# A two-layer decoder on one core: the first loads of two of its attention stages asked for one stage ahead

## What is computed

```python
x = x + _L0_attn_ref(_layernorm(x, axis=-1), L0_attn_w_qkv, L0_attn_b_qkv, L0_attn_w_out, L0_attn_b_out)
x = x + _L0_xattn_ref(_layernorm(x, axis=-1), ctx_1024, ctx_1024, L0_xattn_W_out, L0_xattn_b_out)
x = x + _L0_ffn_ref(_layernorm(x, axis=-1), L0_ffn_Wg, L0_ffn_A, L0_ffn_B)
x = x + _L1_attn_ref(_layernorm(x, axis=-1), L1_attn_Wq, L1_attn_bq, L1_attn_Wk, L1_attn_bk, L1_attn_Wv, L1_attn_bv)
x = x + _L1_xattn_ref(_layernorm(x, axis=-1), ctx_1024, ctx_1024, L1_xattn_wq, L1_xattn_wk, L1_xattn_wv, L1_xattn_wo)
x = x + _L1_ffn_ref(_layernorm(x, axis=-1), L1_ffn_weight, L1_ffn_weight_scale, L1_ffn_bias)
```

## Time and profile before

| what | value |
|---|---|
| median of 3 executions | 3616.16 us |
| the three | 3609.43, 3616.16, 3617.14 us |
| the profiled execution's own time | 3610.95 us |
| its span, first to last instruction | 3609.2 us |
| PE busy, share of the span | 85% |
| DVE, ACT, POOL busy | 75%, 65%, 29% |
| DMA moved | 572.96 MB, mean 159 GB/s |
| expert stage, first DMA to first DMA of the next stage | 1279.53 to 1434.70 us |
| band stage, the same | 1434.70 to 1827.05 us |
| cross stage, the same | 1827.05 to 3427.93 us |

### The profile page before, as it was taken

The page is one execution under the profiler, slowest core; times in us unless marked ns, Lnnn a source line. Parts: engine busy times, 40 slices in busy tenths (PEclk is TensorE's granted clock), DMA queues, the critical chain, the costliest instruction groups (busy, mean ns, idle before and its releaser), DMA issues. The chain is left out here.

```text
span 3609.2 us, 78473 instructions
## 1 busy us (share of the span) xinstructions
PE 3069.9 (85%) x30984; PEld 1833.0 (51%) x31124; DVE 2697.0 (75%) x4017; ACT 2354.9 (65%) x4397; POOL 1062.7 (29%) x1854
## 2 busy tenths in 40 slices
PE   6999989968998944999958898998899989999824
PEld 3747474745665633444435554555555555555411
DVE  4848483767887855344459998889888989899688
ACT  3838383766876634333349988779877888788534
POOL 2232323056346334233322222222222222222122
PEclk9999999989998977999989999999999999999956
DMA  4050505074375175244489999999999999999843
GB/s 154 27 158 18 174 2 151 13 266 120 134 229 169 53 246 202 82 122 121 115 217 192 194 190 203 190 201 198 209 184 194 200 208 188 192 203 192 155 160 126
DMA packets 1308095, 572.96 MB, mean 159 GB/s; under 512 B 1144146, under 2 KB 1230802, under 8 KB 1305172
## 3 DMA queue, kind: packets, MB, share of 16 engines
q1 hardware_dynamic: 1303700, 551.16, 69.4%
q0 software_dynamic: 4032, 16.78, 1.2%
HBM read 174.19 MB, written 109.45 MB: 79 GB/s over the span
## 5 line engine op out<-in xcount | busy, mean ns | idle before, releaser
L2309 DVE TENSOR_REDUCE ca_neg_max<-banks 128x1 f32<-128x1024 f32 x512 | 624.1, 1219 | 82.6 <-PE banks L2087 81.0
L2317 DVE SCALAR_TENSOR_TENSOR ca_halves<-ca_probs,ca_inv,ca_halves 128x1024 f16<-128x1024 f32 x512 | 655.5, 1280 | 39.1 <-ACT ca_halves L2243 29.9
L2235 ACT ACTIVATE ca_probs<-banks,ca_neg_max 128x1024 f32<-128x1024 f32 x512 | 570.5, 1114 | 80.4 <-DVE ca_neg_max L2309 77.5
L2243 ACT ACTIVATE ca_halves<-ca_probs,ca_inv 128x1024 f16<-128x1024 f32 x512 | 587.1, 1147 | 15.8 <-DMA ca_pt<-ca_halves 14.9
L2053 POOL TENSOR_SCALAR ca_inv<-ca_total 128x1 f32<-128x1 f32 x512 | 98.4, 192 | 1153.2 <-ACT ca_probs L2235 1153.2
L2087 PE MATMUL banks<-ca_kt,ca_qt 64*128 64x512 f16 x3072 | 381.0, 381 | 34.3 <-ACT ca_probs L2235 32.8
L2109 PE MATMUL banks<-ca_pt,ca_v 128*64 128x256 f16 x6144 | 387.7, 276 | 16.4 <-DMA ca_pt<-ca_halves 16.2
L2109 PEld LDWEIGHTS banks<-ca_pt,ca_v 128*64 128x64 f16 x6144 | 319.0, 110 | 108.5 <-issue 88.9
L2056 POOL TENSOR_TENSOR ca_inv<-ca_inv,ca_minus_one 128x1 f32<-128x1 f32 x512 | 281.6, 550 | 42.6
L2087 PEld LDWEIGHTS banks<-ca_kt,ca_qt 64*128 64x128 f16 x3072 | 131.3, 95 | 224.6 <-issue 80.8
L2068 PE MATMUL banks<-ca_ct,ca_w 128*128 128x512 f16 x768 | 179.0, 383 | 38.2 <-DMA ca_ct<-ctx_part 23.6
(11 more groups left out here) (306 smaller groups left out, 5737.2 us busy)
## 6 DMA issues: line engine op xcount, KB each, us to landing
ca_w<-ca_w_parts SPq DMA_DIRECT2D x20, 768.0 KB, 5.3
wa_v<-v_rows SPq DMA_DIRECT2D x44, 264.0 KB, 4.6
v_rows<-wa_v_stage SPq DMA_DIRECT2D x32, 264.0 KB, 2.2
wa_x<-in_x SPq DMA_DIRECT2D x32, 256.0 KB, 4.8
wa_ring<-in_x SPq DMA_DIRECT2D x32, 256.0 KB, 3.6
x_after_window_attention<-wa_ring SPq DMA_DIRECT2D x32, 256.0 KB, 3.2
ba_tokens<-wa_tok_turned SPq DMA_DIRECT2D x32, 256.0 KB, 3.6
ba_xt<-ba_tokens SPq DMA_DIRECT2D x32, 256.0 KB, 7.6
```

The source lines that it names most:

```text
L2235: act.activation(probs[:, slot, :], scores(i), ACT.Exp, bias=neg_max[:, slot:slot + 1], accum_out=total[:, slot:slot + 1]).then_inc(exped, 1)
L2243: act.activation(halves[:, i % HALF_SLOTS, 0, :], probs[:, slot, :], ACT.Copy, scale=inv[:, slot:slot + 1]).then_inc(split_hi, 1)
L2309: dve.tensor_reduce(out=neg_max[:, slot:slot + 1], in_=scores(i), axis=X_AXIS, op=ALU.max, negate=True).then_inc(maxed, 1)
L2317: dve.scalar_tensor_tensor(out=halves[:, i % HALF_SLOTS, 1, :], in0=probs[:, slot, :], scalar=inv[:, slot:slot + 1], in1=halves[:, i % HAL ...
```

## The change

Two objects are allocated before the expert stage, in stacks of their own, so that they live across stages. `BandOpening` holds `wv`, its staging tile and the band stage's token tiles; `CrossOpening` holds the cross stage's token tiles, context tiles and weight slots. The expert stage's SP asks for `wv` behind its first residual rows (its batch 1 tokens now follow that), ACT and DVE split it in batch 0 of that stage, and SP asks for the band's first 8 token tiles ahead of the expert's last batch of stores. The band's SP asks for the cross stage's first loads ahead of its own last batch of stores. The two stacks are closed after the band and after the cross stage, each with a clear and a barrier. In the band stage `wq` and `wk` become weights 0 and 1, and the split of `wv` at the head of its ACT and DVE programs goes.

```diff
@@ expert_ffn, SP
                 for t in range(NT):
                     a.load(sp, 0, t)
                 for t in range(NT):
+                    load_residual(sp, n, x_in, 0, t)
+                consts.band.load(sp)
+                for t in range(NT):
                     a.load(sp, 1, t)
-                for t in range(NT):
-                    load_residual(sp, n, x_in, 0, t)
 
                 def before_stores(b, follows):
+                    if not follows:
+                        wait_first_batch_kept(sp, k)
+                        for t in range(NT):
+                            consts.band.a.load(sp, 0, t)
                     if b + 2 < B:
...
@@ expert_ffn, ACT
+                    if b == 0:
+                        consts.band.split_high(act)
@@ expert_ffn, DVE
+                    if b == 0:
+                        consts.band.split_low(dve)
                     out_projection_vector(dve, n, o, k, b)
...
+class BandOpening:
+    def __init__(self, sb, sem, dram):
+        self.source = dram["l1_wv"].rearrange("(k p) n -> p k n", p=P)
+        self.stage = sb("bd_wv_stage", [P, KC, D], F32)
+        self.wv = [sb(f"bd_wv{p}", [P, KC, D], F16) for p in range(2)]
+        self.a = Arrivals(sb, sem, "bd", dram["bd_tokens"])
+        self.loaded, self.high, self.low = sem("bd_wv_loaded"), sem("bd_wv_high"), sem("bd_wv_low")
+
+    def load(self, sp):
+        sp.dma_start(self.stage[:, :, :], self.source).then_inc(self.loaded, 16)
+
+    def split_high(self, act):
+        act.wait_ge(self.loaded, 16)
+        act.activation(self.wv[0][:, :, :], self.stage[:, :, :], ACT.Copy, scale=WS).then_inc(self.high, 1)
+
+    def split_low(self, dve):
+        dve.wait_ge(self.high, 1)
+        dve.scalar_tensor_tensor(out=self.wv[1][:, :, :], in0=self.stage[:, :, :], scalar=WS, in1=self.wv[0][:, :, :],
+                                 op0=ALU.mult, op1=ALU.subtract).then_inc(self.low, 1)
...
+def wait_first_batch_kept(sp, k):
+    for slot in range(k.slots):
+        sp.wait_ge(k.kept[slot], 16 * len(range(slot, NT, k.slots)))
...
@@ band_attention, SP
-                weights(0)
-                for t in range(NT):
-                    a.load(sp, 0, t)
...
-                for m in (1, 2):
+                for m in range(2):
                     weights(m)
...
+                def before_rows(b, follows):
+                    if not follows:
+                        wait_first_batch_kept(sp, k)
+                        consts.cross.open(sp)
...
@@ band_attention, PE
-                pe.wait_ge(w_lo, 1)
+                pe.wait_ge(consts.band.low, 1)
...
+class CrossOpening:
...
+    def open(self, sp):
+        self.load_weights(sp, 0)
+        for p in range(2):
+            self.load_context(sp, 0, p)
+        for t in range(NT):
+            self.a.load(sp, 0, t)
+        self.load_weights(sp, 1)
...
@@ program
+            if name == "expert_ffn":
+                cross_stack, cross_sb, cross_sem = scoped(nc)
+                consts.cross = CrossOpening(cross_sb, cross_sem, dram)
+                band_stack, band_sb, band_sem = scoped(nc)
+                consts.band = BandOpening(band_sb, band_sem, dram)
...
+            if name == "band_attention":
+                band_stack.close()
+            if name == "cross_attention":
+                cross_stack.close()
```

More of the change, by code:

```diff
@@ L77, in __init__ @@
         self.turn, self.x_turn = 0, 0
+        self.band, self.cross = None, None
 def constants(nc, sb, sem):
@@ L1586, in beside @@
                         a.load(sp, b + 1, t)
-                stream_rows(sp, n, x_in, x_out, k, beside=beside)
+                def before_rows(b, follows):
+                    if not follows:
+                        wait_first_batch_kept(sp, k)
+                        consts.cross.open(sp)
+                stream_rows(sp, n, x_in, x_out, k, before=before_rows, beside=beside)
             @block.gpsimd
@@ L1728, in sequence @@
                         if b == 0 and i == 2:
+                            weight_high(0)
+                        if b == 0 and i == 4:
                             weight_high(1)
-                        if b == 0 and i == 4:
-                            weight_high(2)
                         if b == 0 and i == VS:
@@ L1812, in sequence @@
                         if b == 0 and i == 2:
+                            weight_low(0)
+                        if b == 0 and i == 4:
                             weight_low(1)
-                        if b == 0 and i == 4:
-                            weight_low(2)
                         if b == 0 and i == VS:
@@ L1868, with __init__, load_context, pair_of @@
 EARLY_PAIRS = PAIRS - 2
+class CrossOpening:
+    def __init__(self, sb, sem, dram):
+        self.dram = dram
+        self.a = Arrivals(sb, sem, "ca", dram["ca_tokens"])
+        self.ct = [sb(f"ca_ct{p}", [P, KC, S], F16) for p in range(2)]
+        self.w = sb("ca_w", [P, W_SLOTS, 3, 2, KC, P], F16)
+        self.ct_loaded, self.w_loaded = sem("ca_ct_loaded"), [sem(f"ca_stream_loaded{i}") for i in range(W_SLOTS)]
+    def load_context(self, sp, b, p):
+        sp.dma_start(self.ct[p][:, :, :].rearrange("p k s -> p (k s)"),
+                     self.dram["ctx_parts"][p][b * P:(b + 1) * P, :]).then_inc(self.ct_loaded, 16)
+    def pair_of(self, turn):
+        b, at = divmod(turn, PAIRS)
+        return at if b % 2 == 0 else PAIRS - 1 - at
+    def w_place(self, turn):
+        return self.pair_of(turn) % W_SLOTS
+    def w_kept(self, turn):
+        return turn >= PAIRS and turn % PAIRS < W_SLOTS
+    def w_loads(self, turn):
+        return sum(1 for u in range(turn + 1) if self.w_place(u) == self.w_place(turn) and not self.w_kept(u))
+    def load_weights(self, sp, turn):
+        if self.w_kept(turn):
+            return
+        pair, place = self.pair_of(turn), self.w_place(turn)
+        sp.dma_start(self.w[:, place, :, :, :, :].rearrange("p m q k c -> p (m q k c)"),
+                     self.dram["ca_w"][pair * P:(pair + 1) * P, :]).then_inc(self.w_loaded[place], 16)
+    def open(self, sp):
[5 more added lines that the diff above has]
+        self.load_weights(sp, 1)
 def cross_attention(nc, consts, psum, x_in, x_out, dram):
@@ L1875, in cross_attention @@
         n = Residual(sb, sem, "ca", consts, psum)
[L1876 to L1878 removed]
         minus_one = sb("ca_minus_one", [P, 1], F32)
[L1880 to L1909 removed]
+        wo_loaded = sem("ca_wo_loaded")
+        early = consts.cross
+        a, ct, w, ct_loaded, w_loaded = early.a, early.ct, early.w, early.ct_loaded, early.w_loaded
+        pair_of, w_place, w_loads, load_weights, load_context = \
+            early.pair_of, early.w_place, early.w_loads, early.load_weights, early.load_context
         qt = [[sb(f"ca_qt{a}{p}", [P, S], F16) for p in range(2)] for a in range(2)]
@@ L1993, in _ @@
             def _(sp):
-                load_weights(sp, 0)
-                for p in range(2):
-                    load_context(sp, 0, p)
-                for t in range(NT):
-                    a.load(sp, 0, t)
-                load_weights(sp, 1)
                 for t in range(NT):
```

36 lines of the change are left out of this document (6 added, 30 removed).

## The result

| what | before | the change |
|---|---|---|
| executions timed first | 5 | 5 |
| their median | 3611.21 us | 3589.59 us |
| lowest to highest | 3605.95 to 3617.14 us | 3582.96 to 3597.13 us |
| the profiled execution's own time | 3610.95 us | 3588.61 us |
| all executions of this study | 82, mean 3613.3 us | 24, mean 3593.8 us |

The change is faster: 0.9934 of the time before, 95% interval 0.9919 to 0.9949, that is 18 to 29 us. Over all 24 executions of the change the mean is 3593.8 and the median 3595.1, both inside it. The gain in means is 3613.3 − 3593.8 = 19.5 us, with 2.4 us either way (single executions of either kernel scatter with a standard deviation of 5 us; twice √(5.3²/82 + 5.1²/24)). 16.9 were forecast.

A forecast was written before the change was run, and what follows sets the result against it. Most time lies inside stages, but PE's waits for opening loads at the band and cross edges count in full. 9.5 + 8.9 − 0.5 − 1.0 = 16.9 us off 3616.2 gives 3599 us, range 3590 to 3608.

The forecast's parts named there:

- Edge into the band: Band stage opening: with `wv` split and tokens on chip, PE waits only for the masks; gain 9.5 us.
- Edge into the cross stage: Cross stage opening: weights, context and tokens on chip, PE waits only for the barrier; gain 9.4 us before the extra close.
- The price of a start behind a barrier: Both stage openings: PE's delay with nothing else to wait for, between 0 and 0.7 us, taken as 0.1.
- Rival 2: Both stage openings: PE starts late behind the barrier, by 3.3 us; 11.4 us gained, 3605; chance 0.10.
- Extra closes: Ends of band and cross stages: each second stack's clear and barrier costs about 0.5 us.
- The split: Expert stage, batch 0: splitting `wv` on ACT and DVE delays residual adds; cost 1.0 us, between 0 and 1.92.
- Loads at no cost in the expert stage: Expert stage, SP and DMA: early `wv` and band token loads are covered; nothing, or a microsecond or two if cover fails.
- rival 1: Expert stage: 3.1 MB of moved loads lengthens the DMA-bound stage by 8.7 us, leaving 8.2 gained, 3608; chance 0.13.
- Twelve loads in the band's last batch at no cost: Band stage, SP: 5.8 MB of cross-stage loads fit into 39 us of slack before SP's next store; cost nothing.
- Rivals 3 and 4: Cross loop slowed by new tile addresses, 3625, chance 0.04; another wait replacing the loads at one opening, 3608, chance 0.03.
- The clock: Band and cross openings: PE's first products stay slow at granted clock 0.50 despite less idle time; counted as nothing.
- The range: Whole kernel: 3590 (18.9 gained off the lowest run, 3609.4) to 3608, which takes in three of the four rivals.

The follow-up runs named there:

- the third and fourth: The change itself, unedited, timed and profiled again beside the kernel before: medians 3595.70 us of 6 executions and 3598.84 us of 7.

## Why the prediction was right and where it was wrong

- **Edge into the band, −9.5.** Right: PE's first product moved from 10.68 us of the stage to 1.10, 9.6 us, held by the masks; forecast was 1.15. `wq` was not late. In the two profiles of the change whose clock falls as before, the third and fourth, the band stage is 9.8 us shorter (382.4 against 392.2), where 9.0 were forecast with the close.
- **Edge into the cross stage, −9.4.** Right: from 9.49 to 0.19, 9.3 us. The price of a start behind a barrier, bounded by 0 and 0.7 and taken as 0.1, measured 0.19. Rival 2 is out. No run here shows the fetch that the Trainium skill (Runtime: NRT & Kernel Launch, Instruction fetch mechanics) describes behind a taken branch: if there was one, it lies within these 0.19 us or ahead of the barrier, where PE waits anyhow. That such a fetch would now be exposed is not shown.
- **Extra closes, 0.5 each.** Nearly right. At the band's end the two semaphore clears start 0.7 us apart and the two barriers end 0.5 us apart. From PE's last product of the cross stage to the last stage's first instruction it takes 4.40 or 4.41 us in the seven profiles with a second close there and 4.02 or 4.03 in the four without, so that close costs 0.4 us:

```profile
L53 POOLq EVENT_SEMAPHORE_RANGE_CLEAR  x2: 91/221/351, 1814.7 to 1815.4; - x2
L54 SPq EVENT_SEMAPHORE  x2: 17/17/17, 1815.2 to 1815.7; - x2
```

- **The split, +1.0.** 0.6 by the means of five and eight profiles. Its working was right in kind: in the fourth profile the first add comes 1.6 us late (28.2 us), where 1.9 had been worked out, the second 0.5. At the last add of the stage 0.1 us is left there (142.05 against 141.91), 0.5 in the mean of all profiles.
- **Loads at no cost in the expert stage.** Right, and with it rival 1 is out. SP came to the last batch's stores at 131.2 us of the stage (1407.91), where 131.5 had been worked out, and the first keep slid by 1.4 us (by 2.0 to 3.9 in the other profiles with these loads), but the stage's end hardly did:

```profile
1403.98 3.88 SPq L163 DMA_DIRECT2D bd_xt<-bd_tokens  x6
1407.91 7.26 SPq L422 DMA_DIRECT2D x_after_expert_ffn<-ef_ring  x5
1415.47 0.56 SPq L303 DMA_DIRECT2D bd_tokens<-ef_tok_turned  x1
```

- **Twelve loads in the band's last batch at no cost.** Right: SP issued them from 1728.43 to 1739.53, its next store began at 1767.90.
- **Rivals 3 and 4** are out. From the first maximum to the last the cross loop takes 1541.3 us in the mean of seven profiles with the early opening and 1540.0 in the four with the old one, 0.005 us a step, where 0.066 would have eaten the gain. No other wait took over.
- **The clock: "I count nothing here".** Right on average (367.4 against 367.6 us from PE's first to its last product), but the forecast looked at the first products only, and these stay slow. That the falls of the clock later in the stage may come out otherwise in each execution, and move its length by up to 8 us, was not seen.

By the touched stages the sum holds: averaged over all profiles with the old and with the early form, expert +0.6, band 392.2 to 382.7, cross 1600.1 to 1592.0, together −17.0 us against the forecast's −16.9. That the agreement is this close is luck: the split cost 0.4 less than its term, the band gave 0.5 more, and the cross stage gave 0.8 less. The cross stage's first to last product takes 0.9 us longer with the early start (1587.4 against 1586.5); that lies in its loop, and why was not pursued. By the times of 106 executions it is 19.5 with 2.4 either way; taken in three groups, each beside its own executions of before, 21.5, 23.9 and 15.0. The kernel before itself came out 4.9 us lower in a mean of 12 executions than in the 29 beside it, so whether there is a microsecond or two beyond the 17 stays open.

**The step that failed is the range**, as the prediction put it: "from 3590 (18.9 gained, split absorbed, off the lowest run of 3609.4)". Its sum is a microsecond off (with the split absorbed 9.5 + 8.9 − 0.5 are 17.9). It let the size of the gain move by 2 us and took the lowest of three executions for an edge. What it left out is that every execution of either kernel scatters by 5 us, in stages that no edit touches, as the clock falls; these were put at nothing, and gave 5.4 us between the first two profiles. The three times shown, 7.7 us apart, had said as much; 82 executions of before lie between 3596.3 and 3623.3. The median of five such executions has a standard deviation of 2.8 us (1.25 × 5 / √5). Two of these below the 3594 that the sum gives on the profiled execution's footing put the lower end near 3588. That is said afterwards: on the footing that was chosen, 3599, the lower end would have been near 3594. The 9.7 us between the 3599.3 of the sum and the 3589.6 measured are three things: the three executions that the forecast started from had a median 2.9 us above the mean of all 82, the mean gain is 2.6 larger than the sum, and the median of the first five executions lies 4.2 below the mean of the 24, which is chance.

## What to carry to other kernels

Where a stage opens with loads that depend on nothing in the stage ahead, and nothing can be computed meanwhile, nearly the whole wait up to the first product was won here (9.6 of 10.7 us and 9.3 of 9.5), at the price of memory that outlives a stage and of half a microsecond for its close. The forecast of such an edge is simple arithmetic: what does the first product wait for last, once the loads are gone? For the range, look at the scatter between executions before looking at the terms, and do not explain with one profile what a second one does not show.

## What the runs showed of the hardware

- In eight profiles of six kernels PE's granted clock falls at the same places of the band stage, counted from PE's first product, to within 1.2 us (first at 36.8 to 37.9 us, last of six at 275.7 to 276.9), with PE idle ahead of the stage for 6.4 to 16.0 us. In all eight the clock had fallen to 0.50 at 16.7 or 16.8 us ahead of the stage; in the five other profiles it fell at another place, and the falls in the stage were others. Which of the two makes the other, or what makes both, no run shows.
- With the old opening or with PE held back the band stage took 392.0 to 392.4 us (five profiles of four kernels); with PE starting at 1.10 us 377.3 to 386.0 (seven profiles), and 377.3 to 384.7 in four of one kernel, the change.
- One fall of the clock in the tail of a batch costs the band 1.3 to 1.5 us, since PE's products there are on the path (2.11 against 3.43 us).
- PE's first product can start 0.19 us behind a stage's first instruction (the row at 1815.97).
